# Attention output with high and low halves of v side by side: nine products a head become six, and the division by the row sums moves to GpSimd

## The reference, cut to what matters

```
q2 = (q @ wiq.T + biq).reshape(N, H, D).transpose(1, 0, 2)      # N = 384, H = 16, D = 64
k2, v2 = ...                                                    # likewise
scores = einsum('hnd,hmd->hnm', q2, k2) * scale + mask[None]
attn = softmax(scores, axis=-1)
out = einsum('hnm,hmd->hnd', attn, v2)
x = x + (out.transpose(1, 0, 2).reshape(N, 1024) @ wo.T + bo) + mix_ref(xn)
x = x + ffn_ref(layernorm(x))
```

## Time and profile before

| | |
|---|---|
| median of 3 runs | 781.63 us (779.63 to 783.39) |
| the profiled execution | 771.99 us |
| its span, first to last instruction | 770.2 us |
| TensorE's mean granted clock | 0.993 |
| busy: PE, DVE, ACT, POOL | 741.9, 550.0, 387.1, 189.6 us |
| instructions of PE, DVE, POOL | 3977, 1076, 194 |

### The profile page before, as it was taken

How to read it: one execution, slowest core, us unless ns; L and a number is a source line. 1 busy time by engine, 2 the same in 40 slices (tenths; PEclk the granted TensorE clock), 3 DMA queues, 4 the chain that set the end, 5 groups by cost and what they waited for, 6 DMA issues and landing times. The chain is left out here.

```text
span 770.2 us, 10866 instructions
## 1 busy us (share of the span) xinstructions
PE 741.9 (96%) x3977; PEld 660.7 (86%) x3979; DVE 550.0 (71%) x1076; ACT 387.1 (50%) x800; POOL 189.6 (25%) x194
## 2 busy tenths in 40 slices
PE   5998999999999999999997999999999999999998
PEld 4997788999999999988773888888888879998886
DVE  6988684565447998996888787898976677674331
ACT  5433233634336767764766456744774342564220
POOL 5278888888410001011012210000010020000000
PEclk9999999999999999999999999999999999999999
DMA  6664445435533323189854394323243344343431
GB/s 231 230 117 119 111 109 137 110 86 134 174 124 106 103 77 110 34 308 275 258 163 110 83 239 157 137 83 136 86 128 102 114 104 124 131 138 137 137 123 42
DMA packets 37893, 104.55 MB, mean 136 GB/s; under 512 B 12344, under 2 KB 12472, under 8 KB 37584
## 3 DMA queue, kind: packets, MB, share of 16 engines
q1 hardware_dynamic: 24784, 86.76, 33.5%
q0 software_dynamic: 13056, 17.10, 12.5%
HBM read 93.17 MB, written 2.80 MB: 125 GB/s over the span
## 5 line engine op out<-in xcount | busy, mean ns | idle before, releaser
L1217 DVE TENSOR_TENSOR w_lo<-raw,w_hi 128x1024 fp32r<-128x1024 f32 x140 | 170.0, 1222 | 76.4 <-ACT w_hi L927 76.1
L927 ACT ACTIVATE w_hi<-raw 128x1024 fp32r<-128x1024 f32 x140 | 147.3, 1057 | 100.7 <-PE bank L1940 84.5
L1888 PE MATMUL bank<-xn1T,w_hi 128*128 128x384 f32 x416 | 106.8, 337 | 0.0
L1940 PE MATMUL bank<-w_hi,xn3T 128*128 128x512 f32 x288 | 92.0, 393 | 0.0
L795 POOL DMA_INDIRECT count_table<-total,place x48 | 79.0, 1645 | 14.6 <-issue 14.6
L1888 PEld LDWEIGHTS bank<-xn1T,w_hi 128*128 128x128 f32 x416 | 74.3, 188 | 0.1
L1888 PE MATMUL bank<-xn1T,w_lo 128*128 128x384 f32 x208 | 69.6, 335 | 0.0
L1940 PEld LDWEIGHTS bank<-w_hi,xn3T 128*128 128x128 f32 x288 | 54.1, 188 | 11.0
L1888 PE MATMUL bank<-xn4T,w_hi 128*128 128x384 f32 x240 | 61.1, 335 | 0.0
L795 POOL DMA_INDIRECT mask_table<-value,place x48 | 52.5, 1093 | 18.4 <-issue 13.7
L1940 PE MATMUL bank<-w_lo,xn3T 128*128 128x512 f32 x144 | 56.0, 389 | 0.0
(11 more groups left out here) (352 smaller groups left out, 1692.0 us busy)
## 6 DMA issues: line engine op xcount, KB each, us to landing
raw<-weights SPq DMA_DIRECT2D x140, 512.0 KB, 3.3
row_sb<-rows SPq DMA_DIRECT2D x6, 512.0 KB, 5.9
kcat<-kcat POOLq DMA_DIRECT2D x16, 192.0 KB, 2.9
base<-rows POOLq DMA_DIRECT2D x6, 512.0 KB, 13.3
w2r<-w_in SPq DMA_DIRECT2D x1, 2048.0 KB, 10.2
w1r<-w_in POOLq DMA_DIRECT2D x1, 2048.0 KB, 8.7
x_sb<-x_in SPq DMA_DIRECT2D x3, 512.0 KB, 4.8
row_sb<-rows SPq DMA_DIRECT2D x6, 256.0 KB, 5.0
```

Source lines behind the costliest of these rows:

```text
L927: act.activation(w_hi[:, u % RING], raw[:, u % RAW], ACT.Copy).then_inc(hi_split, 1)
L1217: dve.tensor_tensor(w_lo[:, u % RING], raw[:, u % RAW], f(w_hi[:, u % RING]), ALU.subtract).then_inc(unit_split, 1)
L1888: last = pe.matmul(out_of(pr)[:, 0:N], w[pa][:, slot, k * P:(k + 1) * P], TT[src][:, pb, k], start=(k == 0 and m == 0), stop=(k == KD - 1 ...
L1940: last = pe.matmul(out_of(pr)[:], tile[:, pa, k, ts], w[pb][:, at_, j * HALF:(j + 1) * HALF], start=(kk == 0 and j == 0 and m == 0 and nam ...
```

## The change

v2 becomes [node tile][2048]. For each pair of heads it holds four quarters of 64 columns: high of the even head, low of the even head, low of the odd head, high of the odd head. attend of head h now takes the 128 columns of one head, its high and low halves side by side, by probT high and by probT low: six products. The head's own 64 rows of the result hold v high by both parts, the other 64 rows v low by both. VectorE subtracts the high part from its own rows into o_rest, waits for that, and adds the other rows. VectorE still takes the reciprocals of the row sums; the three multiplications by them go to GpSimd, at the step normalise, and so stand in its queue among the kcat copies and ahead of its step at attend of head 15.

```diff
--- before.py
+++ after.py
@@ -453,7 +453,10 @@
         key_part = at("key_part", [P, 2, EC], F16, R3 + 1)
 
         v2f = at("v2f", [P, NT, D], F32, AT + 18)
-        v2 = at("v2", [P, 2, NT, D], F32R, R2)
+        v2 = at("v2", [P, NT, 2 * D], F32R, R2)
+        v2_quarters = v2[:].rearrange("p t (j q c) -> p t j q c", q=4, c=DH)
+        o_rest = row_sb[:, 1, HALF:HALF + N]
+        v2_heads = v2f[:].rearrange("p t (j r c) -> p t j r c", r=2, c=DH)
 
 
         qcat = at("qcat", [P, 2, 2, N], F32R, AT)
@@ -597,6 +600,7 @@
         q_max, q_exp, q_ready = sem("q_max"), sem("q_exp"), sem("q_ready")
         mctx_f, mctx_ready = sem("mctx_f"), sem("mctx_ready")
         s_max, s_exp, p_ready = sem("s_max"), sem("s_exp"), sem("p_ready")
+        r_ready = sem("r_ready")
         k_half, k_twice = sem("k_half"), sem("k_twice")
         base1_ready, base2_ready = sem("base1_ready"), [sem(f"base2_ready{t}") for t in range(NT)]
         ffn_landed = [sem(f"ffn_landed{w}") for w in range(2)]
@@ -863,6 +867,13 @@
                             pool.wait_ge(k_half, s[3] + 1)
                         own, other = slice(64 * r, 64 * r + 64), slice(64 - 64 * r, 128 - 64 * r)
                         pool.dma_start(f(kcat[other, r]), f(kcat[own, r])).then_inc(k_twice, 16)
+                if s[0] == "normalise":
+
+                    h = s[1]
+                    pool.wait_ge(r_ready, h + 1)
+                    for t in range(NT):
+                        pool.tensor_scalar(prob[:, h % 2, t], prob[:, h % 2, t], rsum[:, h % 2, t:t + 1], None,
+                                           ALU.mult).then_inc(p_ready, 1)
                 if s[0] == "degree":
                     wait_emptied(pool, "degree")
                     pool.tensor_tensor(dis[:, 1], dis[:, 0], minus_half[:, 0:NT], ALU.pow).then_inc(dis_ready, 1)
@@ -1018,7 +1029,7 @@
                             sl = slice(c * HALF, (c + 1) * HALF)
                             if name == "v2":
                                 wait_emptied(act, pr)
-                                hi_part(v2[:, 0, t, sl], v2f[:, t, sl])
+                                hi_part(v2_quarters[:, t, 4 * c:4 * c + 4, 0::3], v2_heads[:, t, 4 * c:4 * c + 4])
                             if name == "v":
                                 wait_emptied(act, pr)
                                 hi_part(v_hi[:, t, :, 0:P], vf[:, t].rearrange("p (j c) -> p j c", c=P))
@@ -1457,7 +1468,8 @@
                             for t in range(NT):
                                 wait_emptied(dve, f"{name}.{c}.{t}")
                                 if name == "v2":
-                                    low, high, src = v2[:, 1, t, sl], v2[:, 0, t, sl], v2f[:, t, sl]
+                                    js = slice(4 * c, 4 * c + 4)
+                                    low, high, src = v2_quarters[:, t, js, 1:3], v2_quarters[:, t, js, 0::3], v2_heads[:, t, js]
                                 else:
                                     low, high, src = v_lo[:, t], v_hi[:, t, :, 0:P], vf[:, t].rearrange("p (j c) -> p j c", c=P)
                                 lo_part(low, src, high).then_inc(node_split, 1)
@@ -1550,14 +1562,14 @@
                 if kind == "normalise":
                     h = s[1]
                     dve.wait_ge(s_exp, NT * (h + 1))
-                    link(dve.reciprocal(rsum[:, h % 2], rsum[:, h % 2]))
-                    for t in range(NT):
-                        dve.tensor_scalar(prob[:, h % 2, t], prob[:, h % 2, t], rsum[:, h % 2, t:t + 1], None,
-                                          ALU.mult).then_inc(p_ready, 1)
+                    dve.reciprocal(rsum[:, h % 2], rsum[:, h % 2]).then_inc(r_ready, 1)
                 if kind == "attend":
                     h = s[1]
                     hs = slice(64 * (h % 2), 64 * (h % 2) + 64)
-                    lo_part(TT["o"][hs, 1, h // 2], out_of(f"attend.{h}")[hs, 0:N], TT["o"][hs, 0, h // 2], f"attend.{h}")
+                    other = slice(64 - hs.start, 128 - hs.start)
+                    link(lo_part(o_rest[hs], out_of(f"attend.{h}")[hs, 0:N], TT["o"][hs, 0, h // 2]))
+                    emptied(dve.tensor_tensor(TT["o"][hs, 1, h // 2], out_of(f"attend.{h}")[other, 0:N], o_rest[hs], ALU.add),
+                            f"attend.{h}")
                 if kind == "ffn_mean":
                     w = s[1]
                     pr = f"w_sum.{w}"
@@ -1995,15 +2007,14 @@
                     if h == 0:
                         pe.wait_ge(node_split, 2 * NT)
                     wait_bank(pe, pr)
-                    js = slice(h // 2 * P, (h // 2 + 1) * P)
+                    js = slice(h * P, (h + 1) * P)
 
                     for m in range(NT):
                         pe.wait_ge(act_hi, hi_at[f"pT.{h}.{m}"])
-                        for part in (HI, LO):
-                            pe.matmul(out_of(pr)[:, 0:N], v2[:, part, m, js], probT[:, HI, m], start=(m == 0 and part == HI), stop=False)
+                        pe.matmul(out_of(pr)[:, 0:N], v2[:, m, js], probT[:, HI, m], start=(m == 0), stop=False)
                     for m in range(NT):
                         wait_emptied(pe, f"pT.{h}.{m}")
-                        last = pe.matmul(out_of(pr)[:, 0:N], v2[:, HI, m, js], probT[:, LO, m], start=False, stop=(m == NT - 1))
+                        last = pe.matmul(out_of(pr)[:, 0:N], v2[:, m, js], probT[:, LO, m], start=False, stop=(m == NT - 1))
                     full(last, pr)
                 if kind == "ffn_mean":
                     w = s[1]
```

## The result

The changed kernel takes 809.42 us (median of 4 runs, 807.88 to 810.94), the kernel before 780.63 us in the same comparison (4 runs, 778.11 to 783.39): a ratio of 1.0368, 95% interval 1.0324 to 1.0412. It is slower by 28.8 us.

What follows compares the result with a forecast made beforehand. The prediction took TensorE to bound the attention stage. The stage's +0.9 us, carried into late adds, base1 wait and cold clock, summed to +21.9 us: 781.63 + 21.9 = 803.5, given as 803 us; range 793 to 811.

Steps and rivals of the forecast that it cites:

- rival 2: Attention stage: waits on GpSimd lower TensorE's clock; one fall costs 2.8 us, three make 811 us; chance 0.13.
- The step meant to decide: GpSimd's queue behind the stage: adds wait for the last division, so VectorE stands 20 us for base1.
- So TensorE bounds it: Attention stage: TensorE, busy 20.00 of 20 us, was taken as the bound, with VectorE close behind at 18.18.
- GpSimd's product: Attention division: one 128x384 product by a scalar takes 0.5 us (bounds 0.45 and 0.75), three take 1.5 us.
- The hold: Attention division: GpSimd's SBUF reads are blocked while VectorE's w_lo split runs, ending the three products 1.2 us later.
- The stage: Attention stage: about +0.9 us with GpSimd held at the shared port, about -6.5 us without.
- Start of the adds: Behind the attention stage: the adding DMAs of bo start at 365.5, 24.8 us later than before.
- Length of the adds: Behind the attention stage: the bo and mix_bo adds together take 33.7 us (32.6 to 34.7), completing base1 at 399.2.
- it is hidden behind the wait for base1: Behind the stage: w1r, issued about 385, lands by 394 and its absolute sum ends by 398, before base1.
- The cold clock: Tile steps before the ffn: after idling most of 15 us TensorE's clock falls; the first tile's 18 remaining products take 6.8 us.
- Rival 1: Attention stage: the shared port does not matter, the stage gives -6.5 us; total +13.3 us, 795 us; chance 0.25.
- rival 3: Behind the stage: adds land in time, needing under 14 to 21 us; 774.6 or 782.5 us; chance 0.06.

Runs made afterwards that it cites:

- e1: The changed kernel with both sets of adding DMAs moved earlier in GpSimd's queue, slow division kept: 794.2 us, ratio 1.0161 to the kernel before.
- e8: Six products, division on VectorE, VectorE's second oT operation left out (v-low half not added): 779.62 us, ratio 1.0018 to the kernel before.
- e10: The kernel before with VectorE's w_lo split of q2 units 3 to 7 moved behind the following row maxima: 779.51 us, ratio 0.9964.
- e3: The changed kernel with six products, but the division back on VectorE: 783.79 us, ratio 1.0024 to the kernel before.
- e6: Six products, VectorE divides two of a head's three tiles and ScalarE one: 783.01 us, ratio 1.0046 to the kernel before.
- e7: Six products, ScalarE divides two of a head's three tiles and VectorE one: 779.65 us, ratio 1.0008 to the kernel before.
- e5: The changed kernel with each GpSimd product covering 32 of 384 columns, waits and queue order unchanged: 793.23 us, ratio 1.0137 to the kernel before.
- e2: The changed kernel with w1r issued ahead of the mix_bo adds in GpSimd's queue: 805.56 us, ratio 1.0296 to the kernel before.
- e9: Six products, VectorE divides two tiles and GpSimd one, both sets of adding DMAs early in GpSimd's queue: 784.14 us, ratio 1.0009 to the kernel before.

## Why the prediction was right, and where it was not

The sign was right, and 809.4 us lies inside the range (793 to 811). It is near its upper end, though, and outside the forecast's own 799 to 807: what came is the forecast with the longer products and the fall of the clock that rival 2 had named beside it. That it is as near as 6 us is in part luck, since two large errors of the sum, in the length of the stage and in that of the adds, have opposite signs. The step meant to decide did: GpSimd's queue puts 15 us behind the stage (e1). Of the steps of the sum, several were off, partly in opposite directions.

1. **"So TensorE bounds it"**, the first step, is wrong. A loop of the k2 unit, ScalarE's kcat and 10.4 us of VectorE without a gap sets 15.94 us (e8 and e10). The removed 8.35 us were never on it, and six products gain nothing clear of noise in any version here (e3, e6, e7, e8). VectorE's second oT operation was priced rightly (0.58 us), but booked as room used up; half of them are in the loop, and e3 shows the 0.59 us in the period.
2. **GpSimd's product** was taken at 0.5 us between bounds of 0.45 and 0.75. It takes 1.25. The line through the cast and the select would have given 0.75; neither row has a scalar for each partition, and no run here tests whether that is the reason. Three products are 3.7 us instead of 1.5 and make the division part of a loop of its own (17.2 us).
3. **The hold** exists, and sits where the prediction put it, but for the part of a split that is left when a product starts: 0.54 us a head in the mean, 1.06 at most, instead of 1.2. The Trainium skill, SBUF — State Buffer, section Who interferes with whom, calls the shared pair of ports an exclusive lock, and says that issue order decides who blocks. The rows agree where the split is first (309.48); where GpSimd is first they show a split stretched by 0.24 us (283.76), not one put off until GpSimd's product ends.
4. **The stage** was to lose 0.9 us and lost 13.0. Points 1 to 3 are its causes: 15.96 to 17.2 us in each pair (some 1.2 in each of six, 7.4 in all); the pair of 20.7 us with the lower clock, which took 16.5 before, another 2.9; the pair of 18.1 us, which has the product held for 1.03 us at 309.48, another 0.9; and the heads at both ends the rest. That clock is what rival 2 had named, once instead of three times.
5. **Start of the adds**: 365.5 was predicted, 378.0 measured on the same clock. That is point 4 again, since 12.1 of the 12.5 us are the stage.
6. **Length of the adds**: 33.7 us predicted, 410.56 - 385.20 = 25.4 measured, 8.3 less. The term was mis-sized, and this hid two thirds of the 12.5 us of point 5. The place of the adds goes with it: behind the stage both sets took 26.1 us in e5 too (370.33 to 396.39), while in e1, inside the stage, the first set alone took 19.1 (359.95 to 379.06). The traffic is one difference: w2r's load was done, and SP loads only raw then; that this is the cause was not tested.
7. **"it is hidden behind the wait for base1"**, said of w1r, failed by 2 us: w1r, issued while mix_bo's adds were in flight, took 15.7 us instead of 8.7 (10.8 in e2, ahead of them), and its chain ended at 419.2. The chain that was predicted would have ended at 410.56 + 5.8 + 1.2 = 417.6. e2 shows it binding as soon as w1r is out of the way.
8. **The cold clock** came as predicted: 0.50 from 410 on and 13 products in 5 us. The tiles took 19.0 us against 17.7 for another reason: the sum counted 18 products of the first tile behind the wait, and since TensorE stood for w1q ahead of all tile steps, it was 24. The six more are 6 x 0.227 = 1.4 us; in e2, where the chain is the predicted one, six do run ahead of the wait.

Together: 12.5 - 8.3 + 2.1 (419.65 for the resumption instead of 417.6) + 1.3 (the tiles) = +7.6, on a predicted +21.9: 29.5, and 29.4 were measured. By the medians it is 28.8.

Rival 1 (no hold) is out by the held products, rival 3 (adds in time) by the landings: even 25.4 us are more than the 14 to 21 that it needed. Point 1, the error of mechanism, was not on the list of what could be wrong: the forecast survived it because the six products were worth little in its sum (-1.04 us a pair) beside the queue.

## What to carry to other kernels

An engine that is busy 20 of 20 us can still be waiting: look whether groups of equal products take longer in one place than in another (1.32 against 1.04 us here), whether the loads of weights have gaps that the products hide (19.41 of 20 us here), and whether another engine has one long stretch without a gap between two of its waits. Before work is taken off an engine, write out the loop that sets the period, with each engine's part, and check that the work is in it. And work put into an idle engine's queue delays everything behind it in that queue: read what the queue does next, its DMAs above all.

## What was new about the hardware

GpSimd's multiplication of a 128x384 float tile by a scalar for each partition takes 1.25 us, VectorE's 0.42, ScalarE's 0.60 (e7, median of the 32 at L1006). VectorE's own operation of this kind is slowed from 0.42 to 0.74 us when it starts inside GpSimd's (e9), though each has only one tile to read, and GpSimd's goes from 1.25 to 1.47. Three DMAs that each add 512 KB, one row broadcast over 128 partitions, needed 11.7 and 13.7 us behind the stage (385.20 to 396.88 and 396.88 to 410.56), where the same took 16 to 18 us in the kernel before.
